# Cross-attention and mixed FFN on one core: ScalarE rounds the context's high part two instructions later in the batch step

## The reference

```python
def xattn(q, kv):                      # 16 heads of 16
    qp = heads(q @ w_q + b_q)
    kp, vp = heads(kv @ w_kv + b_kv)
    attn = softmax(qp @ kp.T * SCALE)
    return merge(attn @ vp) @ w_out + b_out

def ffn(h):                            # 8 experts, weights mixed per batch position
    gate = relu(h @ gW1.T + gb1) @ gW2.T + gb2
    g = gate.mean(axis=1)
    W1, b1 = mix(g, eW1), g @ eb1
    W2, b2 = mix(g, eW2), g @ eb2
    return relu(h @ W1.T + b1) @ W2.T + b2

x = x + xattn(layernorm(x), ctx)
x = x + ffn(layernorm(x))
```

## Time and profile before

| what | value |
|---|---|
| median of 3 runs | 972.84 us (971.27 to 977.02) |
| profiled execution, span | 970.9 us, 17228 instructions |
| PE busy | 905.8 us (93%) |
| DVE busy | 485.3 us (50%) |
| ACT busy | 245.3 us (25%) |
| POOL busy | 236.8 us (24%) |
| mean granted TensorE clock | 0.982 |
| context_high, L685 | x16, 821 ns median, 9.3 to 264.3 us |
| context_low, L580 | x16, 1781 ns median, 10.6 to 265.2 us |

### The profile page before, as it was taken

The page is one execution under the profiler, slowest core; times in us unless marked ns, Lnnn a source line. Parts: engine busy times, 40 slices in busy tenths (PEclk is TensorE's granted clock), DMA queues, the critical chain, the costliest instruction groups (busy, mean ns, idle before and its releaser), DMA issues.

```text
span 970.9 us, 17228 instructions
## 1 busy us (share of the span) xinstructions
PE 905.8 (93%) x6250; PEld 748.1 (77%) x6250; DVE 485.3 (50%) x799; ACT 245.3 (25%) x453; POOL 236.8 (24%) x365
## 2 busy tenths in 40 slices
PE   3788898989988699999999999999999999999998
PEld 3667677777776578888888888878888888888887
DVE  6956777787865635555555555553332111111111
ACT  3645566666656310000000000112212001000000
POOL 6533545454532303301100100310103002100000
PEclk9989999999999799999999999999999999999999
DMA  7458656565661163000100010101101101000000
GB/s 185 130 162 204 175 147 178 148 178 140 165 173 45 48 227 102 24 22 22 43 22 22 22 43 22 65 22 45 44 22 50 37 1 44 0 0 0 27 22 27
DMA packets 42934, 74.09 MB, mean 76 GB/s; under 512 B 11514, under 2 KB 33098, under 8 KB 42898
## 3 DMA queue, kind: packets, MB, share of 16 engines
q1 hardware_dynamic: 42898, 73.60, 27.2%
HBM read 56.41 MB, written 17.01 MB: 76 GB/s over the span
## 4 chain that ended last, share of the span: by engine, by line
PE 79%; DMA 7%; DVE 7%; POOL 2%; SPq 2%; issue 2%; ACT 1%; DVEq 0%; ACTq 0%
PE banks L308 37%; PE banks L1511 31%; DMA k_stack<-k_dram 6%; PE banks L1207 3%; PE banks L1230 3%; PE banks L1248 2%; DVE maxima L969 2%; PE banks L1493 1%; DVE xq L940 1%; SPq L371 1%; DVE max_parts L976 1%; SPq L378 1%; DMA k_dram<-k_parts 1%; DVE x_norm L1000 1%; DVE q_stats L929 0%
## 5 line engine op out<-in xcount | busy, mean ns | idle before, releaser
L308 PE MATMUL banks<-w_parts,xt_parts 128*128 128x512 f32 x1344 | 305.5, 389 | 0.0
L308 PEld LDWEIGHTS banks<-w_parts,xt_parts 128*128 128x128 f32 x1344 | 252.0, 188 | 53.4 <-issue 1.1
L1511 PE MATMUL banks<-w_parts,h_high 128*128 (+1 forms) x896 | 240.8, 390 | 1.6 <-DVE h_low L1127 1.6
L1096 DVE SCALAR_TENSOR_TENSOR acc<-banks,gates,acc 128x512 f32<-128x512 f32 x196 | 147.1, 751 | 119.4 <-PE banks L308 119.4
L1511 PEld LDWEIGHTS banks<-w_parts,h_high 128*128 128x128 f32 x896 | 167.2, 188 | 35.9 <-DVE h_low L1127 1.8
L592 POOL TENSOR_TENSOR w_parts<-w_raw,w_parts 128x1024 fp32r<-128x1024 f32 (+1 forms) x32 | 76.4, 2396 | 415.9 <-ACT w_parts L731 415.9
L1121 DVE SCALAR_TENSOR_TENSOR y<-banks,gates,y 128x256 f32<-128x256 f32 x112 | 54.2, 484 | 235.7 <-PE banks L1511 231.4
L1511 PE MATMUL banks<-w_parts,h_low 128*128 (+1 forms) x448 | 138.1, 389 | 0.0
L969 DVE TENSOR_REDUCE maxima<-banks 112x2 f32<-112x750 f32 x128 | 117.6, 933 | 29.8 <-PE banks L1207 27.0
L731 ACT ACTIVATE w_parts<-w_raw 128x1024 fp32r<-128x1024 f32 (+1 forms) x32 | 33.6, 1058 | 354.2 <-PE banks L308 260.8
L694 ACT ACTIVATE probs<-banks 128x448 f32<-128x448 f32 x192 | 100.2, 544 | 30.7 <-PE banks L1230 28.4
(11 more groups left out here) (112 smaller groups left out, 753.1 us busy)
## 6 DMA issues: line engine op xcount, KB each, us to landing
w_raw<-in_w SPq DMA_DIRECT2D x32, 512.0 KB, 3.3
k_dram<-k_parts SPq DMA_DIRECT2D x16, 576.0 KB, 4.0
k_stack<-k_dram SPq DMA_DIRECT2D x32, 288.0 KB
k_stack<-k_dram SPq DMA_DIRECT2D x32, 192.0 KB
c_raw<-in_ctx_t SPq DMA_DIRECT2D x16, 375.0 KB, 5.4
k_stack<-k_dram SPq DMA_DIRECT2D x32, 96.0 KB
b_rows<-gate_dram SPq DMA_DIRECT2D x12, 256.0 KB, 4.8
q_dram<-q_parts SPq DMA_DIRECT2D x16, 168.0 KB, 4.0
```

The lines of the kernel that those rows point to most:

```text
L308: last = pe.matmul(out_ap, left(a, k), right(b, k), start=(n == 0), stop=(n == 3 * tiles - 1))
L1096: dve.scalar_tensor_tensor(out=acc[:, t, 512 * s:512 * s + 512], in0=banks[:, t % NB1, :], scalar=gate_col, in1=base[:, 512 * s:512 * s + ...
L1511: last = pe.matmul(banks[:, t % 2, :], h_part[a][:, t, 2 * c + k, :], w, start=(n == 0), stop=(n == 3 * OT - 1))
```

## The change

In ScalarE's step, `context_high(new)` moves from behind exp 5 to behind exp 6 and `max_copy(nxt,0)`, ahead of exp 7. Nothing else changes: the instruction, its waits and its signal are the same, and no other engine's code is touched.

```diff
@@ -819,12 +819,12 @@
                 exp(s, 3)
                 exp(s, 4)
                 exp(s, 5)
-                if new.exists_from(EARLY):
-                    context_high(new)
                 if last.exists:
                     output_high(last)
                 exp(s, 6)
                 max_copy(nxt, 0)
+                if new.exists_from(EARLY):
+                    context_high(new)
                 exp(s, 7)
                 exp(s, 8)
                 key_copy(new, 0)
```

## The result

The changed kernel takes 984.88 us (median of 6 runs, 980.25 to 986.99), the kernel before beside it 973.79 us. The ratio is 1.0091, with a 95% interval of 1.0065 to 1.0116: 6 to 11 us slower. The medians by themselves lie 11.1 us apart; the ratio stands for 8.9. Run again on another occasion it gave 1.009 (1.0058 to 1.0121). The prediction was +15 us, 987.5 us. The direction, the place and the mechanism of the loss came out as forecast; the size was 4 to 6 us too large.

What follows compares the result with a forecast made beforehand. PE was taken as the bound, in a loop through scores 11 and the key loads. +15.9 loss, -3.5 gain and +2.5 clock make +14.9 us on 970.9, 985.8; with 1.9 for the runs' median 987.5 us, range 979 to 1000.

Steps and rivals of the forecast that it cites:

- The loop: Each step on PE: scores 11, then 9.4 us of SP and DMA, max_scores(nxt,4), then PE's own work, 6.8 us.
- the prediction's third point: SP's key loads start only after scores 11, so a longer PE queue before it lengthens each step by as much.
- Gain, 3.5 us: Before max_transpose on PE: c_low no longer holds DVE's CAST, 0.3 us a step, 3.5 us together.
- Rival C: At DVE's CAST: its hold was the bound, ten steps at 1.6 us, at most 16 us faster, 957 us; chance 0.04.
- Loss, 15.9 us: At key_project(new,0): PE waits for c_low, 1.41 us in ten steps, 0.75 and 1.04 us in steps 2 and 10.
- The clock, +2.5 us: On PE: one in eight of twelve new waits halves the clock, 1.5 falls at 1.7 us; bounds 0 and 20 us.
- Rival A: On PE: the stall costs the clock often; falls after half the waits give 995 us, after each 1006; chance 0.12.
- Rival B: On POOL: c_low is slower in its new place, 2220 ns against 1781, 5.3 us more, 993 us; chance 0.08.
- Rival D: At the next step's max_scores(nxt,4): the wait for keys swallows the stall, +1 us, 974 us; chance 0.08.
- last remark on the rivals: On ACT: c_low not late at all would need c_high to start by +0.14 us; max_rows itself starts at +0.33.

## Why the prediction was right, and where its size was off

**The loop** (scores 11, SP, transfer, max_scores(nxt,4), PE's queue, scores 11): right for the changed kernel, and for half of the steps of the kernel before. In the other half the prediction's third point missed that the held CAST, and not the keys, set when max_transpose could start. The sum doesn't suffer: the gain was read at max_transpose, and a CAST that is free hands these steps back to the keys. From scores 11 at 200.38 to max_scores(nxt,4) at 210.14 it is 9.8 us, as against 9.7 between the same two rows before; the stall lengthened the rest. Steps 17.1 us apart were forecast; steps 3 to 8 began 17.1 to 17.4 us behind the one before.

**Gain, 3.5 us**: right. All twelve steps have max_transpose 1.44 or 1.45 us behind max_scores(nxt,4). Rival C (the whole hold, 16 us) fell as it was argued: DVE's busy time went down by 16.7 us (485.3 to 468.6) and PE saw hardly a quarter of it. Its count was off by one: the CAST was held in steps 2 to 11, and in step 12 the subtraction behind it was, 1.69 us from 265.35.

**Loss, 15.9 us**: nearly right. c_high started at +0.52 (forecast 0.55), c_low at +1.42 (1.45), and key_project at +3.25 (3.37); the hand-over from POOL to PE is 197.69 - 197.63 = 0.06 us and not DVE's 0.13. The shift is 1.29 us in a usual step instead of 1.41, and over the twelve steps, summed from the pairs of rows of both traces, 14.7 us. Less 3.5 this gives +11. The medians say +11.1 and +10.4, the ratios +9 both times, with +11 inside their intervals.

**The clock, +2.5 us**: this is the term that was off most. None of the 24 new waits of 1.04 to 1.15 us in the two traces of the change brought a fall; in both the clock is at 1.00 from 100 to 280 us. Taking the rate of one in eight from the waits for keys was a guess from a single case. Its price, 1.7 us a fall, was a little high as well: the two falls of the kernel before lengthened PE's part by 1.1 us each, those of the kernel with context_high behind exp 7 by 1.5. Rival A's mechanism exists, and the experiment with context_high behind exp 7 shows it at 1.6 us of stall, in four of twelve steps; at 1.1 us it did not set in. What decides is open: the kernel before fell in step 10 behind a wait of 1.28 us, and the one with context_high ahead of exp 3 fell in step 11 (0.50 from 249 us) behind waits of 0.92 and 0.59 us, while the changed kernel kept its clock behind 1.99 us of wait for keys and 1.14 us for c_low in step 2.

**Rival B** (c_low slower in its new place): no, 1.77 us in each of the twelve. bn_stats ran 0.43 us at 196.30 beside c_low and was not held. **Rival D** (the wait for keys swallows the stall): no in steps 1 to 8, where that wait is 1.00 to 1.99 us (0.63 to 2.51 in steps 2 to 8 of the kernel before). In steps 9 to 12 it shrank, to 0.42, 0.91, 0.82 and none, and these steps were 16.0 to 17.0 us apart; summed over steps 2 to 12 the wait for keys went from 12.0 to 11.0 us, so D holds for one microsecond of the loss at most.

**What the text got wrong beside the sum.** Its last remark on the rivals, that c_low wouldn't be late if c_high started by +0.14, is a slip: key_project at +1.96 needs c_high 1.41 us earlier than +0.55, at -0.86. The two experiments with earlier places show that boundary: at 0.95 us earlier a stall of 0.19 us is left.

Four numbers that it reasons with have no row ahead of it; their rows in the trace of the kernel before are (SP; ACT; PE twice):

```profile
193.03 1.23 SPq L378 DMA_DIRECT2D k_stack<-k_dram  x3
...
185.99 0.54 ACT L694 ACTIVATE probs<-banks 128x448 f32<-128x448 f32 x1
...
167.88 0.52 PE L1207 MATMUL banks<-k_stack,q_stack 96*112 96x375 bf16 x2 [1.27 <-DMA k_stack<-k_dram]
...
232.21 0.74 PE L1207 MATMUL banks<-k_stack,q_stack 96*112 96x375 bf16 x2 [1.28 <-DMA k_stack<-k_dram]
```

## What to carry to other kernels

Before an instruction is moved back, compare two slacks: how early its result is now (here 2.3 us), and how much later it will be (here 3.5: from 0.36 us ahead of max_transpose to 3.19 behind it). The difference is paid on the engine that waits, with all that is queued behind, and if that queue feeds the next transfer it is paid in every round. A contention that one sees on a helper engine (here DVE's CAST under POOL's c_low) is worth only what the bounding engine waits for it, 0.3 us of 1.6; and it may be cheaper to move the disturber forward by half a microsecond than to move it out of the way. Where two waits stand one behind the other on the bounding engine, look at their sum over the steps: if it stays the same while they vary, as here 1.35 us, what ends the second one sets the pace, and the first is only room.

## What the runs showed of the hardware

A DVE CAST of 112x8 elements, 0.17 us alone, does not end before a POOL TENSOR_TENSOR of 128x752 that began ahead of it: 1.76 us with the start 0.06 us behind POOL's, 1.08 us with the start 0.72 us behind, to within 0.04 us of POOL's end. In step 12 of the kernel before it was the TENSOR_TENSOR behind the CAST, with two SBUF inputs, that stood for 1.69 us. Three others ran beside the same POOL instruction, in step 7 of the changed kernel, at the length that they have away from it: bn_stats 0.43 us, a reduction from PSUM 0.94, and x_mid, a TENSOR_TENSOR with one operand in PSUM, 0.42. The Trainium skill (GPSIMD Engine Reference, Specifications) names DVE instructions with two SBUF inputs and those in a 2-port mode as the ones that contend with GpSimd. The trace agrees for the one with two SBUF inputs, 1.69 us against 0.17; whether the CAST ran in a 2-port mode no row shows. In these cases POOL had begun first, and only DVE waited: POOL kept its 1.77 us.

The clock of TensorE stayed at its upper level (1.00) from 100 to 280 us of both traces of the change, with a wait of 1.1 us for c_low in each step and one for keys in most, of 1.99 us once and up to 1.4 us else. It fell to 0.50 behind four of the eleven stalls of 1.6 us in the kernel with context_high behind exp 7. A fall lengthened PE's part of a step by 1.5 us there and by 1.1 us in the kernel before.
